# Row statistics of the fp8 stage taken in the stage before, its zeros written by two engines, and the side jobs of the keys in a new order

## The reference

```python
x = x + L0_xattn(_layernorm(x), ctx, ctx, ...)     # attention, 16 heads of 16
x = x + L0_ffn(_layernorm(x), kernel, input_scale, kernel_scale, bias)
x = x + L1_xattn(_layernorm(x), ctx, ...)          # attention, 16 heads of 64, with normalised queries and keys
...
def _layernorm(x, axis=-1, eps=1e-05):
    m = jnp.mean(x, axis=axis, keepdims=True)
    v = jnp.var(x, axis=axis, keepdims=True)
    return (x - m) / jnp.sqrt(v + eps)

def fp8_gemm_optimized(x, input_scale, kernel, kernel_scale):
    x_q = (x / s_in).astype(jnp.float8_e4m3fn)
    k_q = (kernel / s_k).astype(jnp.float8_e4m3fn)
    return jnp.dot(x_q, k_q) * (s_in * s_k)         # then to bfloat16, plus bias
```

## Time and profile before

| | us |
|---|---|
| median of three runs (1672.44 to 1673.75) | 1672.74 |
| the profiled execution | 1676.65 |
| its span, first to last instruction | 1674.9 |
| TensorE matmul busy | 1424.6 (85%) |
| VectorE busy | 1107.1 (66%) |
| ScalarE busy | 762.5 (46%) |
| GpSimd busy | 641.4 (38%) |
| mean granted TensorE clock, share of full | 0.929 |

### The profile page before, as it was taken

How to read it: one execution, slowest core, us unless ns; L and a number is a source line. 1 busy time by engine, 2 the same in 40 slices (tenths; PEclk the granted TensorE clock), 3 DMA queues, 4 the chain that set the end, 5 groups by cost and what they waited for, 6 DMA issues and landing times. The chain is left out here.

```text
span 1674.9 us, 25760 instructions
## 1 busy us (share of the span) xinstructions
PE 1424.6 (85%) x9589; PEld 1204.7 (72%) x9598; DVE 1107.1 (66%) x2383; ACT 762.5 (46%) x1319; POOL 641.4 (38%) x438
## 2 busy tenths in 40 slices
PE   7997768998759999996799997669999999699874
PEld 4786558897549999996677775347888889568622
DVE  7775757987566777774465454676766675567587
ACT  2553554553236777772445333113334443245565
POOL 1461125576123555552132222122666555244100
PEclk9997888999989999998899998889999999799787
DMA  5000000000356777764100000413454443400001
GB/s 190 1 2 5 1 1 1 1 1 1 116 176 202 222 217 223 220 170 92 56 1 1 1 0 1 140 64 108 99 98 98 92 108 51 100 2 1 1 1 50
DMA packets 94177, 122.04 MB, mean 73 GB/s; under 512 B 12300, under 2 KB 79271, under 8 KB 94055
## 3 DMA queue, kind: packets, MB, share of 16 engines
q1 hardware_dynamic: 72935, 91.56, 17.0%
q0 software_dynamic: 21120, 28.85, 9.3%
HBM read 94.95 MB, written 25.43 MB: 72 GB/s over the span
## 5 line engine op out<-in xcount | busy, mean ns | idle before, releaser
L2742 POOL DMA_INDIRECT ch_total<-ch_y,ch_index x64 | 107.4, 1678 | 119.0 <-DVE ch_y L2957 101.5
L1321 POOL DMA_INDIRECT t_total<-t_y,t_index x46 | 98.6, 2143 | 131.2 <-DVE t_y L1442 116.7
L3814 POOL TENSOR_TENSOR L_s<-L_s,L_mx 128x1232 f32<-128x1232 f32 x32 | 76.5, 2390 | 122.6 <-DVE L_mx L3906 122.6
L2872 ACT ACTIVATE ch_silu<-ch_ps 128x512 f32<-128x512 f32 (+1 forms) x68 | 39.0, 574 | 175.0 <-PE ch_ps L836 173.3
L834 PE MATMUL ch_ps<-ch_hT_hi,ch_w_hi 128*128 128x512 f32 (+1 forms) x272 | 106.4, 391 | 11.1 <-DVE ch_hid L2947 7.7
L834 PE MATMUL t_ps<-t_hT_hi,t_w_hi 128*128 128x256 f32 x368 | 106.8, 290 | 6.0 <-DVE t_w_lo L1429 6.0
L834 PE MATMUL t_ps<-t_w_hi,t_act_hi 128*128 128x256 f32 x368 | 105.8, 288 | 0.0
L835 PE MATMUL t_ps<-t_hT_lo,t_w_hi 128*128 128x256 f32 x368 | 105.8, 288 | 0.0
L836 PE MATMUL t_ps<-t_hT_hi,t_w_lo 128*128 128x256 f32 x368 | 105.8, 288 | 0.0
L836 PE MATMUL ch_ps<-ch_hT_hi,ch_w_lo 128*128 128x512 f32 (+1 forms) x272 | 105.1, 386 | 0.0
L835 PE MATMUL ch_ps<-ch_hT_lo,ch_w_hi 128*128 128x512 f32 (+1 forms) x272 | 104.8, 385 | 0.0
(11 more groups left out here) (595 smaller groups left out, 4528.4 us busy)
## 6 DMA issues: line engine op xcount, KB each, us to landing
t_w_in<-in_L_ffn_w1T SPq DMA_DIRECT2D x23, 1024.0 KB
t_w_in<-in_L_ffn_w2T SPq DMA_DIRECT2D x23, 1024.0 KB, 5.7
ch_w_in<-in_L_ffn_w SPq DMA_DIRECT2D x24, 512.0 KB
x<-in_x SPq DMA_DIRECT2D x4, 512.0 KB, 4.7
t_total<-x SPq DMA_DIRECT2D x1, 2048.0 KB
t_rows<-t2d_h SPq DMA_DIRECT2D x1, 2048.0 KB
x<-t_total SPq DMA_DIRECT2D x8, 256.0 KB, 4.8
tb_w<-in_L_xattn_w SPq DMA_DIRECT2D x2, 1024.0 KB, 11.1
```

Source lines behind the costliest of these rows:

```text
L1321: nc.gpsimd.indirect_dma_start(out=total, out_offset=bass.IndirectOffsetOnAxis(ap=index[:, 2 * j + u:2 * j + u + 1], axis=0), in_=y[:, j % ...
L2742: nc.gpsimd.indirect_dma_start(out=total, out_offset=at(s, u), in_=y[:, s % 2, u, :], in_offset=None, compute_op=ALU.add).then_inc(added[s ...
L3814: nc.gpsimd.tensor_tensor(s[:, n % G], s[:, n % G], spread(mx[:, n % G, :], 2, [P, H, KEYS]), ALU.subtract).then_inc(shifted, 1)
```

## The change

- The 16 row statistics of the fp8 stage are taken in the first attention's loop, each behind the centring step of its turn, into the shared tile `k.st`; the fp8 stage begins with the aggregates (`row_moments`, which makes means and inverse roots of statistics that are there already). Likewise the four statistics that the second attention began with are taken at the end of the fp8 stage's queue on VectorE.
- GpSimd writes zeros only to the first batch's half of `wk_vbd`. ScalarE writes the other half and `wk_kbd`, by two activations with a scale of 0 (`zeros`), the first at its queue's start, the second behind the third key job. Its copy for the heads moves behind the variance job.
- On VectorE the weights are rounded ahead of normalising group 1; `key_root` comes behind group 0's rounding and the three `scale` behind group 1's.
- The jobs have a new order and new cuts: 9 before group 0 instead of 14, then 10, 5, 6 and 6. The first job of each group now stands between its transposes and its products on TensorE, and between `turned` and `outputs` on ScalarE. `values_hi` comes behind group 0, `scaled_keys` in group 1 ahead of its outputs.

```diff
@@ -112,10 +112,10 @@
     JOBS = [("key", 0, j) for j in range(3)] + [("variance", 0, 0)] + [("value", 0, j) for j in range(3)]
-    JOBS += [("scale", 0, j) for j in range(3)] + [("fold", 0, f) for f in range(FC)]
-    JOBS += [("bias", 0, j) for j in range(3)] + [("fold", 1, f) for f in range(3)]
-    JOBS += [("bias", 1, j) for j in range(3)] + [("fold", 1, f) for f in range(3, FC)]
-    CUT = (0, 14, 20, 26, 31, 36)
+    JOBS += [("fold", 0, f) for f in range(FC)] + [("scale", 0, j) for j in range(3)]
+    JOBS += [("fold", 1, f) for f in range(4)] + [("bias", b, j) for b in range(B) for j in range(3)]
+    JOBS += [("fold", 1, f) for f in range(4, FC)]
+    CUT = (0, 9, 19, 24, 30, 36)
@@ -142,6 +142,7 @@
+        self.zeroed = sem("wk_zeroed")
@@ -217,7 +218,8 @@
         elif kind == "value":
-            act.wait_ge(self.cleared, 2)
+            act.wait_ge(self.cleared, 1)
+            act.wait_ge(self.zeroed, 1)
             for c in self.chunks(j):
@@ -232,6 +234,11 @@
+    def zeros(self, act, part):
+        out = self.vbd[:, 1].rearrange("p c n -> p (c n)") if part == 0 else self.kbd[:].rearrange("p b n -> p (b n)")
+        self.nc.scalar.activation(out, self.k.ident[:, 0:1].broadcast_to([P, out.shape[1]]), ACT.Copy, scale=0.0
+                                  ).then_inc(self.zeroed, 1)
+
     def heads(self, act):
@@ -240,7 +247,7 @@
         act.wait_ge(self.key_scaled, 3)
-        act.wait_ge(self.cleared, 1)
+        act.wait_ge(self.zeroed, 2)
         for b in range(B):
@@ -265,8 +272,7 @@
     def clear(self, pool):
-        self.nc.gpsimd.memset(self.kbd[:], 0.0).then_inc(self.cleared, 1)
-        self.nc.gpsimd.memset(self.vbd[:], 0.0).then_inc(self.cleared, 1)
+        self.nc.gpsimd.memset(self.vbd[:, 0], 0.0).then_inc(self.cleared, 1)
@@ -684,7 +690,7 @@
-            row_statistics(nc, chain, dve, k.x, range(0, G), st, mv, var, rstd, tmp)
+            row_moments(nc, chain, range(0, G), k.st, mv, var, rstd, tmp)
             for t in range(G):
@@ -964,16 +971,7 @@
             chain = Chain(dve, dve_chain, 0, pad[:])
-            for t in range(NT):
-                chain(nc.vector.bn_stats(st[:, t, :], k.x[:, t, :]))
-            chain.wait_apart()
-            for t in range(NT):
-                ins = nc.vector.bn_aggr(mv[:, t, :], st[:, t, :])
-            chain(ins)
-            chain.wait()
-            chain(nc.vector.tensor_scalar(var[:], mv[:, :, 1], EPS, None, ALU.add))
-            chain.wait()
-            inverse_sqrt(nc, chain, var[:], rstd[:], tmp[:])
+            row_moments(nc, chain, range(NT), k.st, mv, var, rstd, tmp)
             dve.wait_ge(loaded, 64)
@@ -999,14 +997,11 @@
             chain(nc.vector.tensor_scalar(wf[:], w[:].rearrange("p c e -> p (c e)"), inverse[:, 1:2], None, ALU.mult))
+            chain.wait()
+            round_to_fp8(nc, chain, wf[:], wu[:], wf[:], wq[:].rearrange("p c e -> p (c e)"))
+            chain.wait()
+            dve.sem_inc(weights_ready, 1)
             normalise(1)
-            keys.key_root(dve, chain)
-            chain.wait()
-            round_to_fp8(nc, chain, wf[:], wu[:], wf[:], wq[:].rearrange("p c e -> p (c e)"))
-            chain.wait()
-            dve.sem_inc(weights_ready, 1)
-            for j in range(3):
-                keys.scale(dve, j)
             for g in range(NG):
@@ -1026,11 +1021,20 @@
                 nc.vector.tensor_tensor(out, v, unit, ALU.add).then_inc(hq_ready, 1)
+                if g == 0:
+                    keys.key_root(dve, chain)
+                if g == 1:
+                    for j in range(3):
+                        keys.scale(dve, j)
+            biased(NG - 2)
+            dve.wait_ge(x_added, 1)
+            for t in range(G):
+                nc.vector.bn_stats(k.st[:, t, :], k.x[:, t, :]).then_inc(rows_measured, 1)
             dve.wait_ge(keys.vw_hi_ready, 2)
             keys.values_lo(0, 0, FC, keys.vw_lo_ready)
-            biased(NG - 2)
             biased(NG - 1)
             dve.wait_ge(keys.vw_lo_ready, 2)
+            dve.wait_ge(rows_measured, G)
@@ -1055,25 +1059,32 @@
+            keys.zeros(act, 0)
+            for r in range(3):
+                keys.take(act, r)
+            keys.zeros(act, 1)
+            keys.take(act, 3)
             keys.heads(act)
-            for r in range(5):
-                keys.take(act, r)
             act.wait_ge(scales_ready, 1)
             scaled(0)
-            keys.take(act, 5)
+            for r in range(4, 7):
+                keys.take(act, r)
             scaled(1)
-            for r in range(6, keys.CUT[1]):
+            for r in range(7, keys.CUT[1]):
                 keys.take(act, r)
...
                     scaled(g + 2)
+                if g == 1:
+                    keys.scaled_keys(act)
+                own = range(keys.CUT[g + 1], keys.CUT[g + 2])
+                for r in own[:1]:
+                    keys.take(act, r)
                 outputs(g)
+                for r in own[1:]:
+                    keys.take(act, r)
                 if g == 0:
-                    keys.scaled_keys(act)
-                for r in range(keys.CUT[g + 1], keys.CUT[g + 2]):
-                    keys.take(act, r)
-                if g == 1:
                     act.wait_ge(keys.job_taken, keys.taken(keys.JOBS.index(("fold", 0, FC - 1))))
@@ -1101,6 +1112,9 @@
                 ins.then_inc(hqT_psum, 1)
+                own = range(keys.CUT[g + 1], keys.CUT[g + 2])
+                for r in own[:1]:
+                    keys.multiply(pe, r)
                 pe.wait_ge(hqT_ready, g + 1)
@@ -3935,10 +3949,10 @@
                     take(n + AHEAD)
-                if n >= 2 and not a.beside:
-                    next_statistics(n - 2)
                 if a.beside and 1 <= n <= a.beside.DVE_STEPS:
                     a.beside.centre(dve, n - 1)
+                if n >= 2:
+                    next_statistics(n - 2)
                 if normal and n == NT - NormalRows.GROUPS:
@@ -3949,17 +3963,13 @@
             add(NT - 2)
-            if not a.beside:
-                next_statistics(NT - 2)
+            next_statistics(NT - 2)
             if normal:
...
             add(NT - 1)
-            if a.beside:
-                dve.wait_ge(out_added, NT)
-            else:
-                next_statistics(NT - 1)
-                dve.wait_ge(next_ready, NT)
+            next_statistics(NT - 1)
+            dve.wait_ge(next_ready, NT)
```

5 lines of the change are left out of this document (3 added, 2 removed).

## The result

The changed kernel took 1665.61 us (median of 8 runs, 1657.12 to 1672.1), the kernel before in the same session 1674.34 us (8 runs): a ratio of 0.9941, 95% interval 0.9923 to 0.996. By the ratio this is -9.9 us (-6.7 to -12.9), by the two medians -8.7, where -11.2 was forecast. Single runs of the changed kernel differ by up to 15 us, so a sum that is checked to 1 us has to be checked in the stages of the profile, not in the medians.

What follows compares the result with a forecast made beforehand. The fp8 stage, a chain of waits: VectorE sets its first 29.7 us, TensorE and ScalarE the other 38.8. -9.4 (head) - 0.8 (tail) - 1.4 (next stage) + 0.4 (loop's end) = -11.2 us from 1672.74: 1661.5 us, range 1655 to 1669.

Steps and rivals of the forecast that it cites:

- the head's -9.4 us: Fp8 stage's start to the first quantised group f8_hq, VectorE the chain: 29.7 us shortened by 3.4 + 6.0 = 9.4 us.
- (a): Fp8 stage's start on VectorE: the 16 row statistics leave, 5.33 us; aggregates and inverse root stay, 3.56 us.
- (b): Behind the statistics VectorE now waits for four loads, released at 151.6: 3.4 us of the 5.33 won (bounds 0 and 4.0).
- (d): Zeros moved from GpSimd to ScalarE: 2.9 to 3.4 and 2.3 to 2.8 us in ScalarE's idle time, costed at nothing.
- (c): VectorE's key root (3.0 us) and three key scales with waits (3.1 us) move behind groups 0 and 1: 6.0 us won.
- The rule weighed: Loads at the fp8 stage's start: a DMA receipt some 2 us after the last byte would release VectorE at 153.0, sum -9.8.
- The tail, -0.8 us: First quantised group to fp8 stage's end: 4.5 us of matmuls added, 4.7 of waits taken back, 0.6 for fewer joints.
- The clock rival: Late fp8 stage: two TensorE stretches at 1.2 GHz, 2.6 us each, vanish with shorter gaps: -16.4, 1656.3 us; chance 0.10.
- They end near 197, so they are covered: End of VectorE's fp8 queue: four statistics (1.4 us) and the values' low part (3.0 us) end before the last product's copy.
- Next stage -1.4: Second attention's start: its four statistics, 1.41 us, are done inside the fp8 stage: -1.4 us (bounds 0 and -1.5).
- loop 0: First attention's loop: one statistic, some 0.36 us, in fourteen steps fits VectorE's 0.74 us of idle time; cost 0.
- the slower rival: First attention's loop: scores come late, steps of 5.8 us become about 7.3; fourteen make +21, 1682.5 us; chance 0.03.

## Why the prediction was right, and where it was not

The time (1661.5 forecast, 1665.6 measured, within 1655 to 1669) and the sign were right, and the head's -9.4 us came out as -9.3. Of the 4.1 us between the times, 1.6 is the base: the kernel before has a median of 1674.34 over all its runs, where 1672.74 was used. The steps one by one:

- **(a) and (b), 3.4 us.** 3.3 measured between the two profiles (8.89 to 5.63; the wait ended 5.63 us after the start where 5.5 was said). The size is right, the cause was incomplete. I read "it came at 8.9 and waited for nothing" as the statistics' doing. In truth two things led to 8.9 at once: the statistics, and GpSimd's zeroing, which ended at 148.19 + 5.22 = 153.4 and held VectorE's first `tensor_scalar`, `f_var`. With one gone the other still stood: new order with only the statistics moved, 8.83. That the size came out although half of its cause was missing is luck: the zeros were moved for no gain of their own. Two rows of before told it, had I asked why `f_var` on 128x16 took 0.73 us and not 0.17:

```profile
148.19 5.22 POOL L269 MEMSET wk_vbd<- 128x6144 f32 x1
```

```profile
152.71 0.73 DVE L974 TENSOR_SCALAR f_var<-f_mv 128x16 f32<-128x16 f32 x1
```

- **(d) "the zeros cost nothing".** True for ScalarE, whose two activations took 2.76 and 2.26 us (2.9 to 3.4 and 2.3 to 2.8 said) with no one waiting. But the step was priced only where the work went to, not where it came from. Taking it from GpSimd is what makes (b) possible: 3.2 us of head by comparing 23.6 with 20.4.
- **(c) 6.0 us.** 5.9 measured by the new order alone (29.7 to 23.8). And it did more than was said: without it the statistics, with a zeroing in pieces, are worth 0.2 us (29.5), because the old head had TensorE's side jobs as a second bound. The prediction added (b) and (c) as if each would come alone.
- **The rule weighed.** Traffic ended at 147.65 and VectorE was released 0.38 us later (148.03):

```profile
147.40:147.65 0.25, 0.25 (x2) 0.25 (x2) 0.00 (x0) 0.00 (x0) 0.00 (x0) 0.50 0.15 27
147.65:147.90 0.25, 0.25 (x2) 0.25 (x2) 0.00 (x0) 0.00 (x0) 0.00 (x0) 0.50 0.00 0
```

By the receipt of the Trainium skill ("DMA: Bandwidth & Descriptors", "Anatomy of one DMA — SWDGE (gpsimd) path"), some 2 us behind the last byte, the wait would have ended an estimated 7.2 us after the start; this trace disagrees for SyncE's loads, at 5.63. Over eight profiles in which VectorE waited there the release came 4.9 to 6.1 us after the start.

- **The tail, -0.8 us, is the step that failed.** It was computed up to ScalarE's last copy, and there it was better than said: 38.8 us became 35.9 (162.82 to 198.69), -2.9, with waits near those forecast and one stretch at 1.2 GHz where before had two, behind idle times of 3.83 and 3.24 us (in the second, 16 matmuls of 154 columns took 3.93 us and not 2.67). The clock rival thus came half true. The changed kernel's stretch stands behind waits of 1.70 and 0.86 us; its later idle 3.03 us, in the place of the 3.83, brought no fall (granted clock 1.00 from 184 to 190). Busy time by stretch in the changed kernel (columns as in the earlier trace rows; the clock is the last but two):

```profile
162.80:166.00 3.20, 3.04 (x14) 2.40 (x15) 2.77 (x11) 1.99 (x3) 0.00 (x0) 0.50 0.00 0
166.00:169.00 3.00, 3.00 (x12) 2.37 (x11) 2.97 (x7) 1.71 (x5) 0.00 (x0) 0.57 0.00 0
169.00:176.00 7.00, 6.94 (x41) 5.39 (x39) 4.91 (x6) 4.59 (x8) 0.00 (x0) 1.00 0.01 2
```

  But the stage no longer ends there. "They end near 197, so they are covered" was wrong. 197 is on the axis of the kernel before, 50.9 us after the stage's start; the values ended 56.9 us after it (199.27), 6.0 later, and GpSimd's last addition at 202.07, 3.4 us behind ScalarE. Tail +0.5 instead of -0.8. What I had left out were the holds: 1.93 + 1.93 us for the two operations of 2.62, and 0.72 for the values (3.72 against 3.00 before), 4.6 of the 6.0. Another 1.2 lies before the third group, 10.7 us behind the second instead of 9.5, with waits of 1.84 and 0.63 us for the key scales. Before, GpSimd's additions took 3.04 us as well, but VectorE stood idle beside two of them (the second began at 197.75):

```profile
188.07 3.04 POOL L1087 TENSOR_TENSOR x<-x,f_yb 128x1024 f32<-128x1024 f32 x1 [34.65 <-DVE f_yb L997]
```

```profile
192.40 0.69 DVE L1013 TENSOR_SCALAR f_hu<-f_hf 128x1024 int32<-128x1024 int32 x1 [3.28 <-ACT f_hf L1041]
...
200.54 3.00 DVE L260 TENSOR_TENSOR wk_vw_lo<-wk_vw,wk_vw_hi 128x2304 fp32r<-128x2304 f32 x2 [1.73 <-ACT wk_vw_hi L254]
```

  Work that stands in this place is exposed to the holds. With the additions on VectorE the part behind ScalarE falls by 2.2 us. That the whole tail missed by only 1.3 us is luck: one part came out 2.1 us better than said, the other 3.4 us worse.
- **Next stage -1.4, loop 0, end of the loop +0.4.** -1.38 (4.15 to 2.77), steps of 5.80 us in both, +0.46 (2.06 to 2.52 us from the last addition to the stage's start). The idle time fell to 0.43 us where "near 0.4" was said, and with three statistics, 0.98 us a step and so over the 0.74, some steps grew by 0.14 us. The lost pace of the slower rival, 1.5 us a step, did not come.

Together -9.3 + 0.5 - 1.4 + 0.5 = -9.7 us. The -9.9 by the ratio agrees, but its interval, 6 us wide, would have agreed with the forecast's -11.2 as well; it is the stages that tell the two apart.

## What to carry to other kernels

Price an edit that moves work between engines twice: where it lands, and what the old place did to its neighbours. When a removed operation gives nothing, look for a second bound that ends at the same moment, and test edits in combination: here the three parts alone give heads shorter by 5.9, about 0 and (on the new order) 0.6 us, and together 9.3. A tiny operation with a length well above its usual one, and no idle time shown, is a wait in disguise. A row that merges two instructions can hide which of them waited: ask for them one by one. And idle time on an engine can be what shelters it from its neighbour, and it is not free to fill.
